# TensorE's loop of the two pair products: four blocks of each product in a round instead of one

## The reference

```python
# GRU step, 64 times
gi = x @ W_ih + b_ih
gh = h @ W_hh + b_hh
r = sigmoid(i_r + h_r); z = sigmoid(i_z + h_z); n = tanh(i_n + r * h_n)
h_new = (1.0 - z) * n + z * h
# feed-forward over all states, quantised with a scale for each row
qx, sx, sc = _reorder_quantize_x(xf, up_reorder_index)
g = _qlinear(qx, sx, sc, w_gate, ...); u = _qlinear(qx, sx, sc, w_up, ...)
t = silu(g) * u
qt, st, sct = _reorder_quantize_x(t, down_reorder_index)
y = _qlinear(qt, st, sct, w_down, down_reorder_index)
return x + y
```

## Time and profile before

| what | value |
|---|---|
| median of three runs | 2879.51 us |
| span of the profiled execution | 2879.2 us |
| TensorE matmuls busy | 2562.9 us, 89% |
| TensorE weight loads busy | 1681.0 us, 58% |
| VectorE, ScalarE, GpSimd busy | 59%, 40%, 44% |
| mean granted TensorE clock | 0.959 |
| instructions | 154632 |
| DMA | 293.74 MB, 102 GB/s |

### The profile page before, as it was taken

One profiled execution on the slowest core, in us unless ns is written; L12 is line 12 of the kernel. 1 busy time (PEld: TensorE's weight loads), 2 busy tenths in 40 slices (PEclk: granted clock), 3 DMA queues, 4 the chain that ended last, 5 costly groups with the idle time before them and its releaser, 6 DMA issues. The chain is left out here.

```text
span 2879.2 us, 154632 instructions
## 1 busy us (share of the span) xinstructions
PE 2562.9 (89%) x67605; PEld 1681.0 (58%) x67605; DVE 1685.2 (59%) x3398; ACT 1140.6 (40%) x2317; POOL 1262.3 (44%) x598
## 2 busy tenths in 40 slices
PE   2088999998889999999999999999996999999995
PEld 1066777776768888887675564655642444444442
DVE  8852222225632222225646778867592888888887
ACT  1321222225632222224702333323232777777773
POOL 0255666662046666664061363622700333333334
PEclk8599999999999999999999999999998999999998
DMA  6833222224422222226554253442432223232322
GB/s 193 239 85 77 74 73 71 73 71 112 131 63 71 74 73 70 73 71 167 152 135 127 92 151 118 115 156 85 129 143 93 74 84 95 84 95 84 95 63 53
DMA packets 234843, 293.74 MB, mean 102 GB/s; under 512 B 69581, under 2 KB 194023, under 8 KB 233895
## 3 DMA queue, kind: packets, MB, share of 16 engines
q1 hardware_dynamic: 212743, 240.84, 30.6%
q10 hardware_dynamic: 18304, 36.19, 3.6%
q0 software_dynamic: 3680, 15.21, 1.9%
HBM read 231.61 MB, written 60.45 MB: 101 GB/s over the span
## 5 line engine op out<-in xcount | busy, mean ns | idle before, releaser
L1145 PE MATMUL psum<-second_shared 64*32 64x384 f16 x32768 | 1026.0, 324 | 50.2 <-issue 31.3
L1153 PE MATMUL psum<-low_w,low_hot 64*32 64x384 f16 x16384 | 756.5, 324 | 2.0 <-issue 2.0
L1372 DVE TENSOR_SCALAR second_shared<-psum 32x384 f16<-32x384 f32 x496 | 272.3, 549 | 749.1 <-PE psum L1145 741.9
L953 POOL TENSOR_TENSOR low_hot<-first_shared,sum_mask 128x1024 f16<-128x1024 f16 x256 | 499.8, 1952 | 430.1 <-DVE first_shared L1359 183.8
L1145 PEld LDWEIGHTS psum<-second_shared 64*32 64x32 f16 x32768 | 561.5, 93 | 198.0 <-issue 89.8
L947 POOL TENSOR_TENSOR second_shared<-first_shared,whole_mask 128x2048 f16<-128x2048 f16 x128 | 462.5, 3614 | 460.1 <-PE psum L1145 348.2
L1044 ACT ACTIVATE second_shared<-psum 32x384 f16<-32x384 f32 x496 | 239.8, 483 | 801.9 <-PE psum L1145 795.9
L1233 PE MATMUL psum<-low_w,low_hot 64*64 64x384 f16 x12288 | 513.7, 326 | 19.9 <-issue 13.5
L1233 PEld LDWEIGHTS psum<-low_w,low_hot 64*64 64x64 f16 x12288 | 378.3, 108 | 150.4 <-issue 18.4
L310 PE MATMUL psum<-w_x,x_cols 128*64 128x512 f32 (+1 forms) x1856 | 312.0, 495 | 9.5 <-ACT x_cols L280 9.5
L1153 PEld LDWEIGHTS psum<-low_w,low_hot 64*32 64x32 f16 x16384 | 282.5, 93 | 56.8 <-issue 3.1
(11 more groups left out here) (286 smaller groups left out, 2746.6 us busy)
## 6 DMA issues: line engine op xcount, KB each, us to landing
low_w<-w_rows SPq DMA_DIRECT2D x384, 144.0 KB
low_w<-w_rows SPq DMA_DIRECT2D x256, 120.0 KB
second_shared<-w_rows SPq DMA_DIRECT2D x1024, 24.0 KB, 1.9
x_gates<-x_out ACTq DMA_DIRECT2D x58, 384.0 KB, 2.3
xg<-x_gates SPq DMA_DIRECT2D x58, 384.0 KB, 3.2
low_w<-w_rows SPq DMA_DIRECT2D x256, 72.0 KB
low_w<-w_rows SPq DMA_DIRECT2D x384, 48.0 KB
w_rows<-quantised SPq DMA_DIRECT2D x24, 384.0 KB, 4.9
```

The lines of the kernel that those rows point to most:

```text
L953: nc.gpsimd.tensor_tensor(low_hot[:, buf].rearrange("p (s k) b -> p s k b", s=SUBS), low_a[:, slot, bass.ds(c, 1), :, :].rearrange("p a s ...
L1145: last = nc.tensor.matmul(run[m][u][j * Q:(j + 1) * Q, :], whole_hot[rows[u], m, sign, kk, j % 2 * Q:(j % 2 + 1) * Q], whole_w[rows[u], m, ...
L1153: nc.tensor.matmul(run[m][u][j * Q:(j + 1) * Q, :], low_hot[rows[u], m, kk, j % 2 * Q:(j % 2 + 1) * Q], low_w[rows[u], m, at:at + UC], sta ...
L1372: last = nc.vector.tensor_scalar(whole_w[u * B:u * B + Q, m, 0, bq, :], run[m][u][bq * Q:(bq + 1) * Q, :], 1.0 / HIGH_ONE, None, ALU.mult)
```

## The change

TensorE's loop does four blocks of each product in a round instead of one, so it goes round 8 times instead of 32. The counts in the waits are worked out for each block from the new counter n and the block's place d in the round. The order of the blocks, of the matmuls and of the semaphores is what it was, and the streams of the other engines are untouched.

```diff
+                PAIR_ROUND = 4
...
-                            with pe.Fori(0, NBK) as c:
-                                for m in range(2):
-                                    based = c * 2 + (fine_no(t, m, 0) + 1)
-                                    w_ready = c * LOADED + (loaded_before(stage_of(t, m), m) + LOADED)
-                                    whole_ready = c * WHOLE_LOADED + (t * NBK + 1) * WHOLE_LOADED
-                                    hot_ready = c * 2 + (block_no(t, m, 0) + 2)
...
+                            def pair_block(n, d, m):
+
+                                c = PAIR_ROUND
+                                based = n * (2 * c) + (fine_no(t, m, d) + 1)
+                                w_ready = n * (c * LOADED) + (loaded_before(stage_of(t, m), m) + (d + 1) * LOADED)
+                                whole_ready = n * (c * WHOLE_LOADED) + (t * NBK + d + 1) * WHOLE_LOADED
+                                hot_ready = n * (2 * c) + (block_no(t, m, d) + 2)
+                                for value in (based, w_ready, whole_ready, hot_ready):
+                                    pe.compute_val(value)
+                                for u in range(2):
+                                    pe.wait_ge(base_v[u], fine_no(t, m, d) + 1)
+                                    pe.wait_ge(base_v[u], based)
+                                    pe.wait_ge(base_a[u], based)
+                                pe.wait_ge(w_in[m], w_ready)
+                                pe.wait_ge(whole_in[m], whole_ready)
+                                pe.wait_ge(hot_ok, hot_ready)
+                                for kk in range(BK):
+                                    term(m, kk)
+
+                            with pe.Fori(0, NBK // PAIR_ROUND) as n:
+                                for d in range(PAIR_ROUND):
+                                    for m in range(2):
+                                        pair_block(n, d, m)
```

## The result

| kernel | median, us | runs |
|---|---|---|
| before | 2879.05 (2877.49 to 2880.59) | 4 |
| changed | 3357.62 (3350.45 to 3364.60) | 4 |

The ratio is 1.1664, 95% interval 1.1645 to 1.1683: 478.6 us slower. 3405 us was forecast, the range was 3265 to 3520.

What follows compares the result with a forecast made beforehand. TensorE was taken to bound the two pair products. Sixteen rounds of 99.9 us (97.3 fetching, 1.3 way back, 1.3 clock), less 2 x 2.6, gave 1593 against 1068.2 us: 2879.5 + 525 = 3405 us, range 3265 to 3520 us.

Steps and rivals of the forecast that it cites:

- TensorE is the bound in these stretches: In the two pair products, 1068.2 us in all, a microsecond lost or won on TensorE is one of the kernel.
- A page of 256 instructions, asked for one at a time, every 3.86 us: TensorE code not yet on the engine: each page requested on entering the one ahead; 2.61 us of work leaves 1.2 us stops.
- Nothing of the longer body survives: Pair loops: every page of the 24.0 to 24.5 page body is fetched again each round, touching 25.2 pages on average.
- 25.2 x 3.86 = 97.3 us a round: Fetch time of one longer pair-loop round: 25.2 pages touched at 3.86 us each.
- 1.3 us for the way back and 1.3 for the clock: Added per pair-loop round: 1.3 us for the branch back, 1.3 us for one page at the low clock level.
- The branches' 19.7 us: Pair loops: 48 branches removed, each worth at most 0.41 us of TensorE idle time, gain at most 19.7 us.
- The rivals: Other outcomes for the pair products: faster 2860 us (9%), same 2880 (3%), part survives 3268 (6%), clock stays down 3938 (4%).
- Free streaming: Pair products: longer body stays or its pages are fetched further ahead, costing nothing; 19.7 us gained, 2860 us; chance 9%.
- The clock stayed at 0.96 to 0.97: Answers the rival that all pair-product matmuls run at 1.2 GHz: 132.9 us a round, 3938 us; chance 4%.
- No part of a body was seen to survive a round: Answers the rival that six pages of the pair-loop body are found again each round: 91.1 us, 3268 us; chance 6%.

## Why the prediction was right, step by step

- **TensorE is the bound in these stretches.** Right: all but 3.4 us of the change lie in the two products.
- **A page of 256 instructions, asked for one at a time, every 3.86 us.** Right: 3.87 and 3.88 us a packet. Read from six intervals of the first rounds, it held for 397 packets. The rule that a page is asked for only when the one ahead of it is entered is less sure: behind the way back the packets kept their distance although TensorE used up its page later. What asks for a page there is open.
- **Nothing of the longer body survives.** Right: 24.8 packets a round where the term had 25.2. Nothing survived down to a body of 8.55 pages.
- **25.2 x 3.86 = 97.3 us a round.** A round took 769.1 / 8 = 96.1 and 96.3 us. This term alone would have given 16 x 97.3 - 1068 = +489 us, 18 more than the +470.9 of the products; it had 403 packets instead of 397.
- **1.3 us for the way back and 1.3 for the clock.** Mis-sized, both too high: the packets next to a way back come no further apart (3.82 us) than the others (3.87). The stop at the way back is there (3.51 us above), but it is one fetch, already in the 25.2. The branch instruction itself lasts 3.3 to 3.9 us at these 14 places in the trace, and 0.21 us in the kernel before. The low clock behind it is there too and runs inside the fetch's time, which is what the term had wrong: it took the fetch to wait for the slower page. These two terms, less the 5 us taken off for the last rounds, are 36 of the 47 us by which 3405 lay above 3357.6.
- **The branches' 19.7 us.** Not visible. That a boundary's time is not on the path in a loop bound by fetches is argued, not shown.
- **The rivals.** Free streaming would have needed 68 packets or no stops; there are 455, with stops at nearly every page. (The two products had 12 packets before, not the 11 of the prediction; nothing hangs on it.) The clock stayed at 0.96 to 0.97 on average in the products. No part of a body was seen to survive a round. A body of 7.05 pages survived whole in every second round of one product.

## What to carry to other kernels

Before a loop on TensorE is made longer, count the instructions of its body (a matmul counts two, with its weight load): up to some 1550 it stayed on the engine here, but for one refetch in one profiled execution, and at 1805 it no longer did reliably. Beyond that the price is a fetch of 3.8 us for each 256 instructions, in every round. It was hidden where 128 matmuls took 5.2 us, and not where they took 2.61. Look at the first round of the loop and at the instruction queue in the profile before: they show the price of the unrolled version in advance. A boundary's idle time was cheaper to cut by putting waits where their data is first used: 13.8 us here.

## What was not expected of the hardware

- A loop that was not edited can lose time to fetches: the body of 6.05 pages lost 17 us in one profiled execution (9 more packets, a stop of 7.97 us) when longer code ahead of it moved its start to just before a page's end, and did not when it was moved on by 16 instructions. The same place in another program lost nothing, so the cause is open.
- A body of 7.05 pages was found resident in every second round in one product and in none in the other.
- The interval from one page to the next was 3.85 to 3.89 us on average with 8 to 15 GB/s of DMA traffic and 3.87 to 3.88 with 55 to 57.
